# Two row sums of the inner gradient taken apart, in the recurrence of a test-time-training block

## What is computed

```python
def _ln_l2_bwd(Z, tgt, g, b):
    ...
    xh = (Z - mu) / std
    gxh = (g * xh + b - tgt) * g
    return (D * gxh - gxh.sum(-1, keepdims=True) - xh * (gxh * xh).sum(-1, keepdims=True)) / (D * std)

def step(carry, inp):
    W1c, b1c = carry
    xq, xk, xv, et = inp
    Z1 = xk @ W1c + b1c
    grad = _ln_l2_bwd(Z1, xv - xk, g, bb)
    ...
    Z1_bar = xq @ W1c - et * Attn1 @ grad + b1_bar
    W1n = W1c - (last_eta * xk).swapaxes(-1, -2) @ grad
    b1n = b1c - (last_eta * grad).sum(-2, keepdims=True)
    return ((W1n, b1n), xq + _ln(Z1_bar, g, bb, EPS_IN))
```

## Time and profile before

| | |
|---|---|
| median of 3 runs | 630.69 us (630.27 to 630.82) |
| the profiled execution | 633.09 us, span 631.3 us |
| busy, share of the span | PE 80%, DVE 75%, ACT 57%, POOL 53% |
| mean granted clock of PE | 0.72 of full speed |

### The profile page before, as it was taken

One profiled execution on the slowest core, in us unless ns is written; L12 is line 12 of the kernel. 1 busy time (PEld: TensorE's weight loads), 2 busy tenths in 40 slices (PEclk: granted clock), 3 DMA queues, 4 the chain that ended last, 5 costly groups with the idle time before them and its releaser, 6 DMA issues. The chain is left out here.

```text
span 631.3 us, 29708 instructions
## 1 busy us (share of the span) xinstructions
PE 502.7 (80%) x12294; PEld 357.5 (57%) x12294; DVE 471.7 (75%) x1446; ACT 357.4 (57%) x1164; POOL 333.5 (53%) x590
## 2 busy tenths in 40 slices
PE   0389988888248888888887888888788589959996
PEld 0144433444247777787777778777677234427663
DVE  6366888888547888898988998888988337655662
ACT  0344444322336677777777788877676258635321
POOL 1259888877234555555655655555654267530112
PEclk9999999989655555555656655555555679989999
DMA  9201111111570000000000000000000800000113
GB/s 342 82 0 35 37 36 37 39 39 45 121 169 5 2 0 1 0 1 1 0 1 0 2 1 0 1 1 1 1 0 6 287 2 0 2 1 2 69 67 134
DMA packets 11231, 24.73 MB, mean 39 GB/s; under 512 B 3140, under 2 KB 3880, under 8 KB 10920
## 3 DMA queue, kind: packets, MB, share of 16 engines
q1 hardware_dynamic: 11176, 24.09, 12.8%
HBM read 11.50 MB, written 4.19 MB: 25 GB/s over the span
## 5 line engine op out<-in xcount | busy, mean ns | idle before, releaser
L820 PE MATMUL PS<-work 32*32 32x32 f32 x4064 | 82.3, 236 | 43.5 <-DVE work L984 36.3
L820 PEld LDWEIGHTS PS<-work 32*32 32x32 f32 x4064 | 78.5, 150 | 54.6 <-issue 52.0
L1057 POOL TENSOR_TENSOR work<-work,mask 128x256 f32<-128x256 f32 x64 | 46.7, 730 | 90.0 <-DVE work L984 73.5
L809 PE MATMUL PS<-work 64*32 64x64 f32 x2048 | 68.9, 307 | 14.8 <-ACT work L1144 10.3
L809 PEld LDWEIGHTS PS<-work 64*32 64x32 f32 x2048 | 55.1, 162 | 21.7 <-issue 18.7
L832 PE MATMUL PS<-work 32*64 32x32 f32 x2016 | 66.9, 288 | 0.5 <-issue 0.5
L832 PEld LDWEIGHTS PS<-work 32*64 32x64 f32 x2016 | 58.4, 212 | 4.6 <-issue 0.7
L510 PE MATMUL PS<-X,work 128*128 128x512 f32 x128 | 59.2, 606 | 0.1
L1041 POOL TENSOR_TENSOR work<-KP,cst 128x256 f32<-128x256 f32 x64 | 39.3, 613 | 21.6 <-DVE work L946 15.0
L629 POOL TENSOR_TENSOR work<-work 128x512 f32<-128x512 f32 x32 | 43.9, 1373 | 6.7 <-DVE work L572 6.1
L1178 ACT ACTIVATE work<-PS,small 128x128 f32<-128x128 f32 x64 | 23.5, 367 | 39.6 <-PE PS L809 39.6
(11 more groups left out here) (157 smaller groups left out, 1245.9 us busy)
## 6 DMA issues: line engine op xcount, KB each, us to landing
X<-in_x SPq DMA_DIRECT2D x4, 1024.0 KB, 8.1
TK<-KP SPq DMA_DIRECT2D x64, 64.0 KB, 1.9
X<-QP SPq DMA_DIRECT2D x8, 512.0 KB, 8.9
TK<-in_x SPq DMA_DIRECT2D x4, 1024.0 KB, 9.4
out<-TK SPq DMA_DIRECT2D x16, 256.0 KB, 2.3
work<-in_rope SPq DMA_DIRECT2D x2, 512.0 KB, 9.2
cst<-in_consts SPq DMA_DIRECT2D x1, 289.0 KB, 5.0
work<-in_wk SPq DMA_DIRECT2D x1, 256.0 KB, 11.2
```

What stands on the lines that cost most here:

```text
L809: mm = nc.tensor.matmul(PS[HD * a:HD * a + HD, ZB[p], b * ZW:b * ZW + ZW], KT2[p][r:r + 64, k * B + b, :, :].rearrange("p e t -> p (e t)") ...
L820: mm = nc.tensor.matmul(PS[HD * a:HD * a + HD, bank, b * width:b * width + HD], AM[p][HD * a:HD * a + HD, b, part, :, :].rearrange("p e t ...
L1057: nc.gpsimd.tensor_tensor(AM[p].rearrange("p b s e t -> p (b s) e t"), S1[p].unsqueeze(2).broadcast_to([P, 2 * B, E, CS]), mask2.rearrange ...
```

## The change

The reduce over both halves of `YY` becomes two, one for each half, and the multiplication to `cc` becomes two, one for each half of the sums. The first sum is written ahead of the wait for the product `YY[1]`, the mean's coefficient `cc[0]` between the second sum and its coefficient `cc[1]`. `YC` is formed ahead of `WX`. Two semaphores (`my`, `cy`) are new. No other engine's list changes.

```diff
--- before.py
+++ after.py
@@ -753,7 +753,7 @@
                        4, ready=s_pre, at=ORDER)
 
         with nc.Block() as block:
-            names = ("init updw wcopy bcopy kt2 qt2 qr kr khx base qbase corr s1 am z p sq ss sz zc v sd r ts y yp m u u2 "
+            names = ("init my cy updw wcopy bcopy kt2 qt2 qr kr khx base qbase corr s1 am z p sq ss sz zc v sd r ts y yp m u u2 "
                      "yl c w yc gl upd attn zq sqq ssq sdq rq zn zt ot").split()
             q = {n: sem(f"scan_{n}") for n in names}
 
@@ -967,18 +967,22 @@
                     dve.wait_ge(q["y"], c + 1)
                     dve.wait_ge(q["zc"], c + 1)
                     nc.vector.tensor_tensor(YY[:, 1, :, :], YY[:, 0, :, :], ZC, ALU.mult).then_inc(q["yp"], 1)
+                    nc.vector.tensor_reduce(sums[:, 0:B], YY[:, 0, :, :], AX.X, ALU.add).then_inc(q["my"], 1)
                     dve.wait_ge(q["yp"], c + 1)
-                    nc.vector.tensor_reduce(sums, YY.rearrange("p s b d -> p (s b) d"), AX.X, ALU.add
-                                            ).then_inc(q["m"], 1)
+                    nc.vector.tensor_reduce(sums[:, B:2 * B], YY[:, 1, :, :], AX.X, ALU.add).then_inc(q["m"], 1)
+                    dve.wait_ge(q["u"], c + 1)
+                    dve.wait_ge(q["my"], c + 1)
+                    nc.vector.scalar_tensor_tensor(cc[:, 0, :], sums[:, 0:B], -1.0 / HD, lead[:, 0, :],
+                                                   ALU.mult, ALU.mult).then_inc(q["cy"], 1)
                     dve.wait_ge(q["m"], c + 1)
                     dve.wait_ge(q["u2"], c + 1)
-                    nc.vector.scalar_tensor_tensor(
-                        cc.rearrange("p s b -> p (s b)"), sums, -1.0 / HD,
-                        lead.rearrange("p s b -> p (s b)"), ALU.mult, ALU.mult).then_inc(q["c"], 1)
+                    nc.vector.scalar_tensor_tensor(cc[:, 1, :], sums[:, B:2 * B], -1.0 / HD, lead[:, 1, :],
+                                                   ALU.mult, ALU.mult).then_inc(q["c"], 1)
+                    dve.wait_ge(q["yl"], c + 1)
+                    dve.wait_ge(q["cy"], c + 1)
+                    nc.vector.tensor_tensor(YC, YL, bc(cc[:, 0, :]), ALU.add).then_inc(q["yc"], 1)
                     dve.wait_ge(q["c"], c + 1)
                     nc.vector.tensor_tensor(WX, ZC, bc(cc[:, 1, :]), ALU.mult).then_inc(q["w"], 1)
-                    dve.wait_ge(q["yl"], c + 1)
-                    nc.vector.tensor_tensor(YC, YL, bc(cc[:, 0, :]), ALU.add).then_inc(q["yc"], 1)
                     dve.wait_ge(q["w"], c + 1)
                     dve.wait_ge(q["yc"], c + 1)
                     nc.vector.tensor_tensor(GL[p], WX, YC, ALU.add).then_inc(q["gl"], 1)
```

## The result

| | before | changed |
|---|---|---|
| median | 630.76 us (630.27 to 632.08, 4 runs) | 621.3 us (620.3 to 622.96, 4 runs) |
| ratio | 1 | 0.9851 (95%: 0.983 to 0.9872) |
| profiled execution, span | 633.09, 631.3 us | 620.3, 618.5 us |

9.5 us faster by the medians; 620.3 was forecast (10.4 less). The spans of the two profiled executions differ by 12.8. Of that 1.3 us stands ahead of the first Z1 (168.57 against 167.23), where nothing was changed, 1.4 in the first six turns, 9.0 in chunks 6 to 62 and some 1.0 behind them. A second profile of the changed kernel had a span of 620.1.

A forecast was written before the change was run, and what follows sets the result against it. It took the PE-DVE ring through DVE's list from L943 to L984 as the bound. A gain of 0.18 us over 58 turns gave 10.4 us, from 630.69 to 620.3 us; own range 618 to 623, overall 617.5 to 628.

The forecast's parts named there:

- The ring: PE and DVE wait for each other: L984, L820, L943, DVE's list to the next L984; shortening that list shortens each turn.
- DVE's places: Starts after L969's: sums 0.21 and 0.41, `cc[0]` 0.60, `cc[1]` 0.72, YC 0.88, WX 1.09, gradient 1.40 to 1.42 us.
- The separate wait: At L984, a second wait for the newest result costs 0.11 us instead of 0.04; reordering the pair saves 0.07.
- Rival 1: Added waits `my` and `cy` each push what follows by 0.07 us; gain 0.04 a turn, 628.4 us; chance 0.10.
- Gain per turn: DVE's list to the gradient shortens by 0.18 us, 0.07 from reordered waits, the rest from split sums; bounds 0.11 to 0.22.
- Who else could be late: Check of PE ahead of L820: 0.49 us idle, 0.27 left after a 0.22 hand-over, more than the 0.18 gain.
- Rival 2: PE or ACT is the true limit with the same period, DVE waits longer before L943; gain 0, 630.7 us; chance 0.05.
- Turns that count: Of the recurrence's 64 turns, 5 early ones and 1 held up by POOL gain nothing; 58 times 0.18 is 10.4 us.
- YL's cover: POOL's YL ends at 0.70 us, usable by YC at 0.81 after a 0.11 hand-over; cover falls from 0.38 to 0.07.
- The lock: `cc[0]` starts at 0.60 us beside POOL's L1077, running to 0.70 on a shared port; it ends at 0.76, as when free.
- Rival 4: Every DVE instruction is paid in full, without overlap: 0.28 us slower a turn, 16.2 us in all, 646.5 us; chance 0.04.
- Chunk 56: The chunk around 452 us, where POOL's two L1097, 2.48 us in all, hold DVE up; gain counted as 0.

## Why the prediction was right, and where its terms were off

The mechanism was right: a shorter DVE list in the ring that carries the state, by overlapped sums and by a carried wait. That the time came within 1.0 us of the forecast is in part luck, since two of its terms were off in opposite directions (below).

- *The ring* L984, L820, L943 and DVE's list: right. The list from Z1 to the gradient went from 3.72 to 3.52 (medians), and the gap before Z1 stayed 1.10.
- *DVE's places*: right to 0.03 us. The overlapped starts held for new instructions (0.21, 0.20, 0.19), and the small ones took 0.16.
- *The separate wait*: right, and shown by itself from both sides (0.11 to 0.04 when the add carries the newest result's wait; YC 0.05 earlier when it carries `cy`'s). Rival 1 had 0.07 twice on top. Of the two added waits only `cy` costs, and that was in the sum.
- *Gain per turn*: 0.18 forecast, 0.195 measured.
- *Who else could be late*: this step failed in one turn of four. It took PE's spare time from an ordinary turn (0.49 idle before L820) and found 0.27 left. The hand-over of 0.22 in the same sum (303.97 to 304.19) was taken from another turn, one with a loop-back; an ordinary one is 0.10. The row of that L820 already shows the loop-back, with 0.62 of idle in place of 0.49, and so does the turn of the earlier trace rows, whose gap before Z1 is 1.22 and not 1.10:

```profile
304.19 0.65 PE L820 MATMUL PS<-work 32*32 32x32 f32 x32 [0.62 <-DVE work L984]
```

Behind a loop-back PE had nothing left even before, in 10 of the 13: it started L820 mostly 0.61 to 0.67 after L874's end. Rival 2, a second ring of the same period, had been given 0.05 for the whole; for a quarter of the turns it was true.

- *Turns that count*: so not 58, but 58 less the 13 loop-backs after chunk 6, 45. 45 times 0.195 is 8.8 us, where 58 times 0.18 was 10.4. The two errors pull against each other. Chunks 6 to 62 hold 42 of these turns, which gives 8.2 us; measured there, the recurrence lost 9.0 us in one profile (272.21 to 263.20) and 7.8 in the other (264.38). The difference goes along with the quick turns (10 and 5, against 3 before), of 0.2 us each. In the 0.6 us ahead of their Z1 the granted clock was 1.00, and 0.50 ahead of nearly all others (53 of 53 before, 42 of 46 and 48 of 51 in the changed kernel's two profiles). So up to 1.4 us of the 9.0, and 0.4 of the 7.8, came with the clock and not by the shorter list itself; whether the change brings more such turns is not shown.
- *YL's cover*: 0.07 forecast with a hand-over of 0.11. The run with a later YL showed DVE 0.03 behind POOL's end, so the hand-over was some 0.03 at most and the cover 0.12 or more. The 0.11 of the earlier trace rows was read as the price of a hand-over, and here it was a third of that.
- *The lock*: no cost here, as forecast; the price if the two fall differently is 0.13 a turn (shown in the kernel before). The rule of the Trainium skill, "SBUF — State Buffer", section "SBUF: two separate sides", on the port pair that a GpSimd op and a Vector op with two SBUF inputs share exclusively, is borne out by `cc[1]` in the run with a later YL: 0.36 instead of 0.16, ending 0.01 after POOL's. Its strict reading (begin only afterwards) is not: this one and the held L976 of the kernel before end 0.01 and 0.02 after the other, less than their own length.
- *Rival 4*: out, by the overlapped starts (0.21 and 0.20) with the sums apart alone. Its rule from the Trainium skill, "VectorE: DVE Perf Modes", section "The DRAIN you can't avoid", goes on there to say that a next op that is not held starts earlier. The prediction left that half out, and it is the half that these starts bear out.
- *Chunk 56* (both `pre` operations): I counted 0; its list went from 5.75 to 5.60, 0.15 less.
- *Two slips in the sums*: rival 4's 16.2 us on 630.7 make 646.9, not 646.5, and the slow end of the forecast's own range was worked out with 0.13 a turn where the bound in the text is 0.11 (624.3 us, not 623). Neither touches the forecast.

What stays open is which part of PE's 0.61 us at a loop-back is the branch and which the reading of code, and why the two profiles of one kernel differ in the number of quick turns.

## What to carry to other kernels

Where a ring of engines carries a state, write down one turn with start times, and then a second one for each kind of turn (the loop-back, the chunk with extra work): a cover computed on the ordinary turn says nothing about the others. A row from one kind of turn must not be subtracted from a row of another. Before an instruction with two waits ask which is met last and write that one first; here that alone was 0.08 of the 0.195 a turn, and it needed no split. Splitting a reduce pays where the halves become ready at different times and the engine starts independent instructions before the last has ended: 0.07 for the sums, and 0.05 for the order that two separate coefficients allow.

## What the runs showed of the hardware that I had not expected

- A separate wait met last costs 0.07 us more than a carried one, and the order of two source lines decides it (3.6 us of 631, ratio 0.9947).
- Over a loop-back of PE 0.61 to 0.66 us pass from the last matmul group to the first, where 0.30 passed without one in the changed kernel (and there the gradient was what PE waited for). A loop of 4 chunks (168 matmuls, each with its weight load, in a chunk) moved 0.38 MB of code in all; loops of 6 and 12 moved 1.74 MB and made the kernel 63 and 51 us slower than the changed one.
- A DVE instruction of 4 columns (0.16 us) that started beside a GpSimd one of 0.40 lasted until that one's end: 0.36.
